# A macaron block on one core: order of transposes, copies and preparation in the attention loops

## Chip, cores, metric

The kernel runs on one core of a Trainium2 chip. The metric is the device time of one execution in microseconds; the median of three runs counts.

## The reference

The input x has 8 batches of 1024 tokens with 128 features, in f32. Three parts follow one another: half a feed-forward part (FFN), causal attention, and half an FFN again with the same weights.

```python
x = x + 0.5 * ffn(layernorm(x))
x = x + attention(layernorm(x))
x = x + 0.5 * ffn(layernorm(x))

def attention(z):                       # per batch, D = 128, 1024 tokens
    Q, K, V = z @ Qw, z @ Kw, z @ Vw
    s = Q @ K.T / sqrt(D) + causal_mask
    return softmax(s) @ V

def ffn(z):                             # 16 experts of 64, 4 chosen per token, one shared of 128
    cw = routing weights (sigmoid scores, groups, top 4, scaled)
    return sum_e cw[:, e] * (relu(z @ W1[e].T) ** 2 @ W2[e].T) + relu(z @ Ws1.T) ** 2 @ Ws2.T
```

## The kernel before

Each engine has one program, written out by hand; engines meet only by semaphores. An FFN runs over 16 groups of 512 tokens and 9 chunks of hidden units each. Most products are split into three f32r products (`split3`, lines 1371 to 1375). The second FFN's first groups (0 to 3) are prepared during the attention by `start_ffn(k)`, with k = 8(b-6) + s.

The attention runs over batches b = 0..7, and each batch has 8 slots s. Slot s handles the query tile t = `ORDER[s]` of (7, 3, 6, 2, 5, 1, 4, 0), each tile being 128 queries wide against (t+1)*128 keys. The even slots hold the wide tiles 7, 6, 5, 4 (`LATE`), the odd ones the narrow tiles 3, 2, 1, 0 (`SOON`). In a slot:

- TensorE writes the scores (`score`, L1567), into one of two PSUM homes; it waits for the exp of two slots before.
- VectorE takes the row maximum (`row_max`, L1246 or L1244), and L1248 shifts it for wide tiles.
- ScalarE takes the exp with its row sum (`exp`, L759).
- For a wide tile ScalarE casts the probabilities to f16 (`prob_hi`, an L572 copy into `shared`), GpSimd writes the remainder (`prob_lo`, L544), and SP transposes both by DMA (`prob_transpose` of SP, L352) into `wb`. TensorE uses them in `pair` (L1610 to L1612).
- For a narrow tile TensorE transposes the f32 probabilities (`prob_transpose`, L1585) into one PSUM bank, `tp_ps`, and ScalarE copies them out (`pT_copy`, an L572 copy into `w_raw`). Each transpose waits for the copy of the one before. TensorE uses the four tiles in `mix` (L1594), which the next batch's first `pT_copy` waits for, since it overwrites their home.

The results of `mix` and `pair` are copied (`uT_copy`, into `s_sb`), multiplied by Vw (`values`, L1626) and added to x on VectorE (`finish`, L1284). Beside this each loop prepares the next batch: transposes of the normalised tokens (L1559), `z_hi_copy` and `z_lo_part`, the product with Qw Kw^T (`q_product`, the `m_hi` rows of L1373 to L1375), `q_hi_copy` and `q_lo_part`, and ScalarE normalises the batch after next (`normalise` of the attention, L779, four instructions a half).

ScalarE's `start_ffn` does, for the FFN groups: half of the normalising (L586), `x_copy` (into `x_f`), `x_hi_copy` (into `x_hi`), a sigmoid by exp (L623) and `wT_copy` (into `wT`). Copies of all kinds stand on L572, so they are told apart by their tiles. TensorE's `start_ffn` transposes the normalised group (L1404), makes the logits (L1412) and transposes the routing weights (L1432). SP stores and spreads these (L363, L380), in the same queue as the DMA transposes. k = -22 to -19 fall in b=3, -14 to -11 in b=4, 0 to 7 in b=6 and 8 to 15 in b=7.

Of the kernel before, what the change touches and what calls it, by code (L numbers as in the profile page):

```python
# [118 lines left out]
def macaron_kernel(nc, x, Qw, Kw, Vw, Wg, bias_corr, W1, W2, Ws1, Ws2, out):  # L119
    B, S, D = x.shape  # L120
# [8 lines left out]
    QT = S // P  # L129
# [18 lines left out]
    with ExitStack() as ctx:  # L148
# [75 lines left out]
        SOON = ORDER[1::2]  # L224
# [346 lines left out]
        def _(sc):  # L571
# [157 lines left out]
            def attention(close_ffn, start_ffn, lead_ffn):  # L729
# [66 lines left out]
                def run():  # L796
                    for b in range(B):
                        for s in range(QT):
                            if b == 0 and s == 0:
                                close_ffn()  # L800
                            if b > 0 and s == 0:
                                pT_copy(b - 1, SOON[2])
                            if b > 0 and s == 2:
                                pT_copy(b - 1, SOON[3])
                            if b > 0 and s == 4:
                                uT_copy(b - 1, 1)
                            if b > 0 and s == 6:
                                uT_copy(b - 1, 0)
                            if b + 1 < B and s in (0, 2):
                                z_hi_copy(b + 1, s // 2, prep_ps)  # L810
                            exp(b, s)
                            if s in (5, 6):
                                pT_copy(b, SOON[s - 5])
                            if b + 1 < B and s in (4, 6):
                                q_hi_copy(b + 1, (6 - s) // 2, prep_ps)
                            if b + 2 < B and s == 4:
                                normalise(b + 2, 1)
                            if b + 2 < B and s == 6:
                                normalise(b + 2, 0)
                            if s % 2 == 1:  # L820
                                prob_hi(b, ORDER[s - 1])
                            start_ffn((b - (B - 2)) * QT + s)

                    pT_copy(B - 1, SOON[2])
                    pT_copy(B - 1, SOON[3])
                    start_ffn(16)
                    for r in range(3):
                        sc.wait_ge(A.p16_in[r], 16 * B)
                    lead_ffn(0)
                    lead_ffn(1)  # L830
                    uT_copy(B - 1, 0)
                    start_ffn(17)
                    lead_ffn(2)
                    uT_copy(B - 1, 1)
                    lead_ffn(AHEAD - 1)
# [532 lines left out]
        def _(pe):  # L1368
# [183 lines left out]
            def attention(close_ffn, start_ffn, lead_ffn):  # L1552
# [92 lines left out]
                def run():  # L1645
                    pe.wait_ge(m_ready, 1)
                    for b in range(B):
                        new = b + 1 < B
                        for s in range(QT):
                            if b > 0 or s > 1:  # L1650
                                score(b, s)
                            if b == 0 and s == 0:
                                close_ffn()
                            if s == 0:
                                if new:
                                    wait(pe, A.qlo_done[0], b + 1)
                                    z_transpose(b + 1, 0, prep_ps)
                                if b > 0:
                                    pair(b - 1, PAIRS[0], HQ, PAIRS[0] + 2)
                            if s == 1 and b > 0:  # L1660
                                prob_transpose(b - 1, SOON[3])
                            if s == 1 and b > 1:
                                values(b - 2, 0)
                            if s == 2 and new:
                                pe.wait_ge(A.zlo_done[0], b + 2)
                                z_transpose(b + 1, 1, prep_ps)
                            if s == 3 and b > 0:
                                pair(b - 1, PAIRS[1], 0, PAIRS[1] + 2)
                            if s == 4 and new:
                                q_product(b + 1, 1, prep_ps)  # L1670
                            if s == 5:
                                if b > 0:
                                    mix(b - 1)
                                prob_transpose(b, SOON[0])
                            if s == 6:
                                if new:
                                    pe.wait_ge(A.qlo_done[1], b + 2)
                                    q_product(b + 1, 0, prep_ps)
                                prob_transpose(b, SOON[1])
                                if b > 0:  # L1680
                                    values(b - 1, 1)
                            if s == 7:
                                prob_transpose(b, SOON[2])
                                pair(b, PAIRS[0], 0, HQ)
                            start_ffn((b - (B - 2)) * QT + s)

                    b = B - 1
# [56 lines left out]
```

## Time and profile before

| | us |
|---|---|
| median of 3 runs | 685.28 |
| the three runs | 685.28, 686.0, 681.53 |
| the profiled execution: its own time | 686.61 |
| its span | 684.8 |
| TensorE busy | 640.4 (94%) |
| VectorE busy | 559.1 (82%) |
| ScalarE busy | 549.7 (80%) |
| GpSimd busy | 521.7 (76%) |

The attention loops lie between about 278 and 446 us of the span. In a timeline row the columns are start, length, engine, line, operation, tiles written and read, shapes and the number of merged instructions; in brackets stands the engine's idle time before it and what ended it. The lengths of matmuls include a modelled end, so that the next often starts before it.

### The profile page before, as it was taken

Reading aid. Unit: us, or ns where it says so; the run is one execution under the profiler, and the core shown is the slowest. Engines: PE = TensorE matmul, PEld = TensorE weight load, DVE = VectorE, ACT = ScalarE, POOL = GpSimd, SP = SyncE. Lnnn points to the kernel's source line nnn. Section 1 sums busy time; section 2 is a strip of 40 time slices with the busy share of each in tenths; the row PEclk is TensorE's granted clock in tenths of the full one; section 3 lists DMA queues with packets and bytes.
Section 4 is the critical chain, followed back from the end, with each engine's and each line's share of the span. In section 5 each row is a group of like instructions: output and inputs, shape, how many; then the busy total and the mean of one; then the engine's idle time right before and its main releaser. Section 6 shows DMA issues by size and latency. Waiting matters only on the chain.

```text
span 684.8 us, 15211 instructions
## 1 busy us (share of the span) xinstructions
PE 640.4 (94%) x3395; PEld 493.8 (72%) x3395; DVE 559.1 (82%) x2576; ACT 549.7 (80%) x1171; POOL 521.7 (76%) x411
## 2 busy tenths in 40 slices
PE   4689999999999997699998998999999999999997
PEld 3457777777777765578776886777777777777775
DVE  5888989989899897767767768779889889898863
ACT  3478879898888874778887786769888898988975
POOL 3378889899998885665655546558899998999975
PEclk9699999999999999999999999999999999999999
DMA  9866677865777650334544435886867878768782
GB/s 245 194 139 128 140 160 151 167 130 129 161 158 165 134 124 1 59 74 76 96 81 78 74 76 96 162 161 123 171 143 159 176 170 174 160 142 187 167 172 76
DMA packets 107801, 92.05 MB, mean 134 GB/s; under 512 B 59488, under 2 KB 73456, under 8 KB 107760
## 3 DMA queue, kind: packets, MB, share of 16 engines
q1 hardware_dynamic: 105552, 91.00, 63.6%
q10 hardware_dynamic: 2208, 0.59, 0.4%
q8 instruction: 16, 0.26, 0.2%
q14 instruction: 25, 0.20, 0.1%
HBM read 72.70 MB, written 5.24 MB: 114 GB/s over the span
## 4 chain that ended last, share of the span: by engine, by line
PE 69%; DVE 13%; ACT 6%; issue 6%; DMA 3%; POOL 2%; SPq 0%; POOLq 0%; ACTq 0%; DVEq 0%
PE psum L1373 18%; PE psum L1374 17%; PE psum L1375 17%; PE psum L1446 3%; DVE w_raw L1246 3%; DMA wb<-scratch 2%; PE psum L1404 2%; PE psum L1458 2%; DVE zn L1272 1%; PE psum L1420 1%; DVE s_sb L1100 1%; PE psum L1412 1%; PE psum L1610 1%; ACT s_sb L759 1%; PE psum L1612 1%
## 5 line engine op out<-in xcount | busy, mean ns | idle before, releaser
L452 POOL TENSOR_TENSOR shared_r<-shared,shared_r 128x512 fp32r<-128x512 f32 x256 | 326.6, 1298 | 57.7 <-ACT shared L642 55.1
L1100 DVE SCALAR_TENSOR_TENSOR s_sb<-psum,wb 128x512 f32<-128x512 f32 x256 | 175.6, 687 | 47.4 <-DMA wb<-scratch 22.4
L641 ACT ACTIVATE shared_r<-s_sb 128x512 fp32r<-128x512 f32 x256 | 160.0, 625 | 46.3 <-DVE s_sb L1100 43.0
L642 ACT ACTIVATE shared<-s_sb 128x512 f32<-128x512 f32 x288 | 177.6, 619 | 20.0 <-DVE s_sb L1100 20.0
L1373 PE MATMUL psum<-x_hi,w_hi 128*128 128x512 f32 x288 | 126.3, 439 | 1.2 <-issue 0.9
L1373 PE MATMUL psum<-shared_r,w_hi 128*128 128x512 f32 x256 | 115.6, 452 | 1.2 <-POOL shared_r L452 1.0
L1375 PE MATMUL psum<-x_hi,w_lo 128*128 128x512 f32 x288 | 114.2, 396 | 0.0
L1374 PE MATMUL psum<-x_lo,w_hi 128*128 128x512 f32 x288 | 114.0, 396 | 0.0
L1374 PE MATMUL psum<-shared_r,w_hi 128*128 128x512 f32 x256 | 101.7, 397 | 0.0
L1375 PE MATMUL psum<-shared_r,w_lo 128*128 128x512 f32 x256 | 101.0, 395 | 0.0
L544 POOL TENSOR_TENSOR shared<-s_sb,shared 128x1024 f16<-128x1024 f32 (+3 forms) x32 | 56.7, 1771 | 44.3 <-ACT shared L572 44.3
L1373 PEld LDWEIGHTS psum<-x_hi,w_hi 128*128 128x128 f32 x288 | 54.7, 190 | 21.9 <-issue 8.2
L1374 PEld LDWEIGHTS psum<-x_lo,w_hi 128*128 128x128 f32 x288 | 54.6, 190 | 18.1 <-issue 7.2
L1375 PEld LDWEIGHTS psum<-x_hi,w_lo 128*128 128x128 f32 x288 | 54.5, 189 | 11.9
L1373 PEld LDWEIGHTS psum<-shared_r,w_hi 128*128 128x128 f32 x256 | 48.7, 190 | 19.2 <-issue 5.7
L586 ACT ACTIVATE xn<-x_sb,shift,roots 128x128 f32 (+1 forms) x128 | 55.4, 481 | 3.7 <-DVE shift L939 3.7
L1375 PEld LDWEIGHTS psum<-shared_r,w_lo 128*128 128x128 f32 x256 | 48.3, 188 | 11.6
L1374 PEld LDWEIGHTS psum<-shared_r,w_hi 128*128 128x128 f32 x256 | 49.0, 191 | 4.7 <-issue 0.2
L471 POOL TENSOR_TENSOR roots<-powers,neg_half 128x8 f32<-128x8 f32 x28 | 46.0, 1641 | 7.8 <-DVE powers L1080 5.5
L1246 DVE TENSOR_REDUCE w_raw<-psum 128x1 f32<-128x1024 f32 (+3 forms) x32 | 32.6, 1020 | 22.5 <-PE psum L1579 22.3
L458 POOL TENSOR_TENSOR x_lo<-x_f,x_hi 128x512 fp32r<-128x512 f32 x32 | 41.6, 1299 | 7.2 <-ACT x_hi L572 7.2
L759 ACT ACTIVATE s_sb<-psum,w_raw 128x1024 f32<-128x1024 f32 (+3 forms) x32 | 30.6, 955 | 16.3 <-DVE w_raw L1248 16.3
(170 smaller groups left out, 1372.3 us busy)
## 6 DMA issues: line engine op xcount, KB each, us to landing
wb<-scratch SPq DMA_DIRECT2D x128, 512.0 KB, 7.9
out<-x_sb SPq DMA_DIRECT2D x16, 256.0 KB, 9.9
x_sb<-in_L_attn_x SPq DMA_DIRECT2D x4, 256.0 KB, 6.2
scratch<-wT SPq DMA_DIRECT2D x32, 32.0 KB, 1.9
w_raw<-in_L_ffn_W ACTq DMA_DIRECT2D x1, 512.0 KB, 6.0
w_raw<-in_L_ffn_W SPq DMA_DIRECT2D x1, 512.0 KB, 6.6
wb<-shared SPq DMA_TRANSPOSE x32, 4.1
w_raw<-in_L_ffn_Ws ACTq DMA_DIRECT2D x1, 64.0 KB, 8.7
```

The costliest lines, as they stand in the source:

```text
L452: nc.gpsimd.tensor_tensor(g_lo[:, j % RING, :], g_f[:, j % RING, :], g_hi[:, j % RING, :].bitcast(F32), ALU.subtract).then_inc(F.glo_done, 1)
L458: nc.gpsimd.tensor_tensor(x_lo[:, u, :], x_f[:, u, :], x_hi[:, u, :].bitcast(F32), ALU.subtract).then_inc(F.xlo_done, 1)
L471: nc.gpsimd.tensor_tensor(roots[:], powers[:], neg_half[:, 0:2 * TG], ALU.pow).then_inc(F.rstd_done, 1)
L544: nc.gpsimd.tensor_tensor(prob16[t][:, :, 1, :], whole, prob16[t][:, :, 0, :], ALU.subtract).then_inc(A.plo_done, 1)
L586: ins = nc.scalar.activation(xn[:, t, :], x_sb[:, bass.ds(g * TG + t, 1), :].rearrange("p t d -> p (t d)"), ACT.Identity, bias=shift[:, t: ...
L641: nc.scalar.activation(g_hi[:, j % RING, :], s_sb[:, j % RING, :], ACT.Square)
L642: nc.scalar.activation(g_f[:, j % RING, :], s_sb[:, j % RING, :], ACT.Square).then_inc(F.sq_done, 1)
L1100: ins = nc.vector.scalar_tensor_tensor(s_, h_, 0.0, wb[:, u, c, :], ALU.max, ALU.mult)
L1246: nc.vector.tensor_reduce(raw_max[:, t:t + 1], src, AX.X, ALU.max, negate=True).then_inc(A.raw_max_done, 1)
L1373: mm(out_, l_hi, r_hi, start=start, stop=False)
L1374: mm(out_, l_hi, r_lo, start=False, stop=False)
L1375: return mm(out_, l_lo, r_hi, start=False, stop=stop)
```

## The change

On TensorE the transposes of tiles 3 and 2 stand first behind the scores of slots 5 and 6: ahead of `mix`, and ahead of the wait for and the work of `q_product`. On ScalarE the copy of tile 2 stands ahead of slot 6's exp instead of behind it, and `start_ffn` stands ahead of the attention's `normalise` and of `prob_hi` instead of behind them. No instruction is added or removed.

```diff
@@ ScalarE, attention, run @@
-                            if b > 0 and s == 6:
-                                uT_copy(b - 1, 0)
+                            if s == 6:
+                                if b > 0:
+                                    uT_copy(b - 1, 0)
+                                pT_copy(b, SOON[1])
                             if b + 1 < B and s in (0, 2):
                                 z_hi_copy(b + 1, s // 2, prep_ps)
                             exp(b, s)
-                            if s in (5, 6):
-                                pT_copy(b, SOON[s - 5])
+                            if s == 5:
+                                pT_copy(b, SOON[0])
                             if b + 1 < B and s in (4, 6):
                                 q_hi_copy(b + 1, (6 - s) // 2, prep_ps)
+                            start_ffn((b - (B - 2)) * QT + s)
                             if b + 2 < B and s == 4:
                                 normalise(b + 2, 1)
                             if b + 2 < B and s == 6:
                                 normalise(b + 2, 0)
                             if s % 2 == 1:
                                 prob_hi(b, ORDER[s - 1])
-                            start_ffn((b - (B - 2)) * QT + s)
@@ TensorE, attention, run @@
                             if s == 5:
+                                prob_transpose(b, SOON[0])
                                 if b > 0:
                                     mix(b - 1)
-                                prob_transpose(b, SOON[0])
                             if s == 6:
+                                prob_transpose(b, SOON[1])
                                 if new:
                                     pe.wait_ge(A.qlo_done[1], b + 2)
                                     q_product(b + 1, 0, prep_ps)
-                                prob_transpose(b, SOON[1])
                                 if b > 0:
                                     values(b - 1, 1)
```

## Rows read from the trace of the kernel before

**Rows 1.** Busy time by stage, the loop of b=3: stretch and length, then each engine.
```profile
337.12:359.70 22.58, 21.06 (x149) 17.12 (x147) 16.48 (x59) 18.45 (x42) 13.22 (x11) 1.00 0.40 76
```
**Rows 2.** Waits of TensorE, 278 to 450 us: total, times, longest.
```profile
PE psum L1585 <- ACT w_raw L572: 5.7, 9, 1.0
...
PE psum L1412 <- ACT x_f L572: 2.0, 3, 0.8
```
**Rows 3.** Timeline of TensorE, b=2, slots 6 and 7.
```profile
329.26 0.48 PE L1373 MATMUL psum<-z_hi,m_hi 128*128 128x512 f32 x1
...
330.09 0.52 PE L1585 MATMUL psum<-ident,shared 128*128 128x128 f32 x3
330.45 1.06 PE L1626 MATMUL psum<-vw,s_sb 128*128 128x128 f32 x8
...
332.47 0.41 PE L1585 MATMUL psum<-ident,shared 128*128 128x128 f32 x2 [0.61 <-ACT w_raw L572]
```
**Rows 4.** Timeline of ScalarE, b=2, the copies pT3 and pT2.
```profile
329.36 0.58 ACT L572 ACTIVATE w_raw<-psum 128x512 f32<-128x512 f32 x1
...
331.82 0.50 ACT L572 ACTIVATE w_raw<-psum 128x384 f32<-128x384 f32 x1
```
**Rows 5.** Timeline of TensorE, b=3, slots 5 to 7.
```profile
346.56 2.38 PE L1594 MATMUL psum<-w_raw,zn 128*128 128x512 f32 x8
348.77 0.60 PE L1585 MATMUL psum<-ident,qk_all 128*128 128x128 f32 x4
350.21 1.06 PE L1412 MATMUL psum<-wgT,x_f 128*128 128x16 f32 x8 [0.84 <-ACT x_f L572]
...
354.91 0.41 PE L1585 MATMUL psum<-ident,shared 128*128 128x128 f32 x2 [0.17 <-ACT w_raw L572]
```
**Rows 6.** Timeline of ScalarE, b=3: normalising, the x copy, pT3.
```profile
348.04 1.64 ACT L779 ACTIVATE zn<-x_sb,w_raw 128x128 f32<-128x128 f32 x4
349.57 0.58 ACT L572 ACTIVATE x_f<-psum 128x512 f32<-128x512 f32 x1
...
350.50 0.60 ACT L572 ACTIVATE w_raw<-psum 128x512 f32<-128x512 f32 x1
```
**Rows 7.** TensorE in b=0, then stages; behind POOL the granted clock.
```profile
289.78 0.52 PE L1585 MATMUL psum<-ident,shared 128*128 128x128 f32 x3 [0.87 <-ACT w_raw L572]
...
291.67 0.59 PE L1585 MATMUL psum<-ident,shared 128*128 128x128 f32 x2 [1.02 <-ACT w_raw L572]
...
281.52:284.93 3.41, 1.87 (x11) 1.59 (x11) 2.65 (x6) 2.62 (x6) 2.58 (x3) 1.00 0.01 2
...
288.35:291.76 3.41, 1.52 (x11) 1.01 (x10) 1.01 (x3) 3.41 (x9) 1.32 (x1) 1.00 0.61 113
291.76:295.17 3.41, 3.41 (x16) 2.57 (x17) 0.69 (x1) 3.02 (x9) 2.62 (x4) 0.50 0.59 113
```
**Rows 8.** b=6 and b=7: TensorE, ScalarE, DMA transposes of tiles 6 and 4.
```profile
419.08 0.41 PE L1585 MATMUL psum<-ident,shared 128*128 128x128 f32 x2 [0.90 <-ACT w_raw L572]
...
440.69 0.41 PE L1585 MATMUL psum<-ident,shared 128*128 128x128 f32 x2 [0.91 <-ACT w_raw L572]
...
450.99 0.27 PE L1610 MATMUL psum<-wb,zn 128*128 128x256 f16 x1
...
442.88 0.60 ACT L572 ACTIVATE x_f<-psum 128x512 f32<-128x512 f32 x1 [1.36 <-PE psum L1404]
...
L352 SPq DMA_TRANSPOSE wb<-shared x1: 2543/2543/2543, 435.5 to 435.5; - x1
DMA to landing us min/median/max: 5.1/5.1/5.1
...
L352 SPq DMA_TRANSPOSE wb<-shared x1: 1922/1922/1922, 443.0 to 443.0; - x1
DMA to landing us min/median/max: 6.1/6.1/6.1
```
**Rows 9.** The page's DMA issues: KB each, median us from issue to landing.
```profile
wb<-scratch SPq DMA_DIRECT2D x128, 512.0 KB, 7.9
```

## The prediction

> **What bounds the kernel now.** I read the page first. Its busy shares and its slices (TensorE 94%, a slice near 0.9 almost everywhere) say that TensorE sets the pace of both feed-forward parts and that the attention between them is where it has gaps. Then the busy time of one attention loop: the loop of batch b=3 takes 22.58 us of which TensorE is busy 21.06, ScalarE 18.45 and VectorE 16.48 [rows 1]. So no engine is full and TensorE comes nearest. There are eight such loops and the change touches only them. Next the waits of TensorE between 278 and 450 us: the transposes wait for a copy out of their PSUM bank nine times, 5.7 us in all, and the FFN logits wait for the copy of x three times, 2.0 us [rows 2]. Those two rows are what the change can reach. All else it can do only by making something earlier that TensorE then uses.
>
> I name the slots of a loop by s=0..7. The narrow tiles' transposes are T3 (tile 3, s=5), T2 (tile 2, s=6), T1 (tile 1, s=7) and T0 (next loop), their ScalarE copies pT3, pT2, pT1, pT0. One PSUM bank holds each in turn, so T2 waits for pT3 and T1 for pT2.
>
> **Change 1, T3 ahead of mix (s=5): 0 by itself.** pT3 also waits for mix (it overwrites what mix reads), so pT3 starts when both are done, as before. TensorE does the same work in another order.
>
> **Change 2, T2 ahead of the q product and pT2 ahead of exp (s=6).** Take b=2, which has no FFN work in these slots. Before: q product at 329.26, T2 at 330.09, values at 330.45, then TensorE runs free and sits idle 0.61 until T1 at 332.47, which pT2 released [rows 3]; pT2 starts at 331.82 and ends at 332.32 [rows 4] behind an exp. After: T2 would start at 329.26, but pT3 runs from 329.36 to 329.94 [rows 4], and the distance from a copy's end to the released matmul is 332.47 - 332.32 = 0.15 us. So T2 starts at 330.09 again, and 330.09 - 329.26 = 0.83 us of wait stands before it. The same work (q product, T2, values, score 7) that began at 329.26 and ended at 332.47 - 0.61 = 331.86 now begins 0.83 later and ends at 332.69. A matmul that waits for nothing starts about 0.16 before the modelled end of the one before it (T2 started at 330.09 with 0.52, the next at 330.45) [rows 3], so T1 starts at about 332.5. pT2 no longer waits for the exp, so it ends before 332.32 and is no longer the last. T1 moves from 332.47 to 332.5: nothing. A wait of 0.6 is removed and one of 0.8 is put before T2, against 0.2 of overlap that the stall hid. The stall stays, since pT3 is set by ScalarE's own row of work (exp, q copy, four normalisings, exp), which the change does not shorten. The same holds for b=1 and b=5. Bounds for the three loops: between a loss of 0.2 and a gain of 0.2 each; I take 0.
>
> In b=0 there is no mix and no values product. T2 stands at 289.78 and T1 at 291.67, with waits of 0.87 and 1.02 [rows 7]. T2 keeps its time (pT3), then q product 0.83, score 7 about 0.43: T1 at about 291.4. Gain 0.3 (0 to 0.6).
>
> **Change 3, the next stage's preparation ahead of normalise (b=3, b=4, s=4).** The logits of FFN group 0 wait 0.84 us for the x copy [rows 5], which starts at 349.57 behind four normalisings of 1.64 us from 348.04 [rows 6]. Now the copy starts at 348.04 and ends near 348.6. mix (346.56, 2.21 us to T3 at 348.77) and T3 (0.36) are done at 349.13 [rows 5], so the logits start there instead of at 350.21: 1.08 earlier, because T3's modelled end hid 0.24. From there to the end of score 7 TensorE took 354.91 - 0.17 - 350.21 = 4.53 us [rows 5]. In the new order about 0.1 comes on top, a wait of T2 for pT3 (350.50 to 351.10 [rows 6], which ScalarE's sum of work leaves where it is): the end is at 349.13 + 4.63 = 353.76, T1 about 0.16 before that, 353.6 against 354.91. Gain 1.3, of which the removed stall before T1 is a part. What is late next is pT3, not the logits. ScalarE's normalising is only 0.6 later and its reader is the next loop but one. b=4 repeats b=3 with the same two waits (0.84 and 0.17): 1.3 again. The times behind T1 in the next loop are led by TensorE and VectorE chains that start from its scores, so I let the gain stand. Bounds: 0.4 to 1.4 each.
>
> **Change 4, the last two loops (b=6, b=7).** Here preparation is moved not past normalise (there is none) but past the odd slots' half-precision copy of the wide probabilities, prob_hi. Gain side: T1 of b=6 waits 0.90 [rows 8]; with pT2 ahead of exp about 0.55 of it goes, and since VectorE leads the start of b=7, I count 0.4. T1 of b=7 waits 0.91 and could come 1.1 earlier. But the pair product right behind it needs the DMA transpose of tile 6, issued at 435.5 and landed 5.1 later, 440.6, while T1 stands at 440.69 [rows 8]. So that gain is hidden by the transfer. Loss side: x_hi of group 1 (a 512-wide copy as that at 442.88, 0.60 us) [rows 8] goes ahead of prob_hi of tile 7 and pushes GpSimd's chain, hence that transpose, back by 0.5. And in the last slot the x copy of group 3, which waits for TensorE until 442.88 [rows 8], goes ahead of prob_hi of tile 4. The transpose of this tile was issued at 443.0, GpSimd's 1.4 us and the cast's 0.7 after the cast's start near 440.8. Now the cast starts near 443.5, so prob_hi, GpSimd's low part, SP's DMA transpose (landed 6.1 after its issue, 449.1 [rows 8]) and SP's last load of routing weights queued behind it all move by about 2.7. Landing at 449.1 + 2.7 = 451.8 against the pair product's start at 450.99 [rows 8]: up to 0.8 late. In b=6 half the normalising of group 2 likewise goes ahead of prob_hi of tile 4; its transpose is used only in slot 3 of the next loop, and I put the loss inside the bounds. Together b=7 loses 0.5 (from a loss of 2.5, if the transpose meets the weight loads, to a gain of 0.4).
>
> The Trainium skill (page "TensorE: Matmul & The Clock Gate", section "Architectural detail: the array is 16× 32×32, not 1× 128×128") says ScalarE takes its queue strictly in order while TensorE can pull weight loads ahead. By that rule the blocked x copy holds all behind it, and change 4 has its loss; were it not so, the loss would be 0 and the sum 3.3.
>
> **Sum**: 0.3 + 0 + 1.3 + 1.3 + 0.4 - 0.5 = 2.8 us. The profiled execution took 686.61 us (span 684.8), so its like would take 683.8. The median of the runs shown is 685.28, 1.3 below the profiled one, so I predict 685.28 - 2.8, about 682.4.
>
> **The clock.** Between 288.35 and 291.76 TensorE was busy 1.52 us, with the two waits of b=0 in it, and the clock of the next stretch, to 295.17, was 0.50, that is 1.2 GHz; the stretch from 281.52, with 1.87 us busy, was followed by full clock, 2.4 GHz [rows 7]. The change takes the second of the two waits away. If the low stretch goes with it, its 3.41 us of work take half: 1.7 less. I leave it out of the sum: these rows show one case, and not that the wait was its cause.
> The same page of the Trainium skill ("HAM oscillation — how this bites in real kernels") has the clock fall after one long idle gap. Here it fell after waits of at most 1.02 us [rows 7], so the trace does not bear the rule out; by the rule there would be nothing to win, by the rows 1.7.
>
> **Rivals.** (a) The low stretch goes: 682.4 - 1.7 = 680.7. For it: TensorE does more just before it. Against: the first wait stays and grows. (b) The gains of b=3 and b=4 are eaten by later waits, above all TensorE's for VectorE in the next loop: both at their lower bound of 0.4, 1.8 less, 684.2. For it: VectorE carries routing work in b=4; against: its chain starts from TensorE's first score. (c) Slower: the blocked ScalarE queue in b=7. If the delayed transpose (issued at 445.7) runs beside the 512 KB weight loads and takes as long as these do, 7.9 us [rows 9], it lands at 453.6, 2.6 after the pair product was due; the last weight load, behind it on SP, is then needed as much later and costs nothing more. With x_hi's 0.5, and nothing won in b=6, 3.1 are lost against the gains of 0.3 + 2.6: 685.28 + 0.2 = 685.5. It decides from a landing at 453.4; every microsecond beyond that is one more. (d) Before T2 of b=0 the idle time now stands in one piece, 0.87 + 0.83 [rows 3, 7], and the clock falls for one more stretch: 682.4 + 1.7 = 684.1.
>
> **Chances.** Forecast (681.5 to 683.5) 0.50; (a) 0.20; (b) 0.15; (c) 0.07; (d) 0.08. The runs of the kernel before lie 4.5 us apart, so the range must take more than the terms: 679.3 to 685.9, with all four rivals in it. One per cent is 6.9 us, about what a measurement of this kernel tells from no change. The waits that the change reaches [rows 2] sum to 7.7 us, so faster by over 1% needs nearly all of them and the clock: 0.05. Slower by over 1% needs twice rival (c): 0.03. Within 1%: 0.92.
>
> **What would show it.** Right: the T1 waits on the copy are gone in all eight loops and a wait of 0.6 to 0.9 stands before T2 in b=1, 2, 5; the logits' wait of 0.84 is gone in b=3 and b=4, whose loops are 1.0 to 1.3 shorter; loops 1, 2 and 5 are as long as before; prob_hi of tile 4 in b=7 starts behind the x copy, near 443, and its transpose lands within 1 us of the pair product. Wrong: loops 1, 2 and 5 get shorter by over 0.3 (then pT3 is not what holds T2), or loop 7 with the start of the second FFN grows by over 1.5.

## The result, and the profile after

| | before | after |
|---|---|---|
| median of 20 runs each, taken side by side | 685.0 | 679.94 |
| lowest and highest | 681.2 to 687.84 | 677.11 to 682.79 |
| the profiled execution: its own time | 686.61 | 682.48 |
| its span | 684.8 | 680.7 |

The ratio is 0.994, with a 95% interval of 0.9923 to 0.9957: about 4.1 us less, where 2.8 were forecast. (It is formed from the means, 684.24 and 680.0; the medians are 5.06 apart.) The two profiled executions are also 4.1 apart (686.61 - 682.48), so their traces can be set against each other. All times are in us.

Busy times by engine, from the page after, are within 1.2 us of those before (TensorE 641.5, VectorE 558.4, ScalarE 549.4, GpSimd 521.8): nothing was removed, the time is idle time.

To find the place I measured each loop from the start of its first exp (tile 7) to that of the next; the last one up to the product of the second FFN that follows TensorE's wait of 0.85 to 0.88 behind the attention's last work (457.56 before, 453.51 after). This table is worked out from those starts, for all kernels of this study:

| kernel | b=0 | 1 | 2 | 3 | 4 | 5 | 6 | 7 |
|---|---|---|---|---|---|---|---|---|
| before | 20.30 | 19.33 | 19.81 | 22.58 | 23.95 | 19.87 | 21.31 | 32.73 |
| after | 20.08 | 19.20 | 19.71 | 21.06 | 22.55 | 19.79 | 20.42 | 33.10 |
| e1_preparation_only | 20.29 | 19.30 | 19.83 | 21.47 | 22.84 | 19.87 | 20.57 | 33.28 |
| e2_transposes_only | 21.13 | 19.21 | 19.71 | 22.09 | 23.54 | 19.78 | 21.30 | 33.24 |
| e3_t2_behind_q | 17.94 | 18.78 | 19.04 | 20.97 | 22.44 | 19.09 | 20.43 | 33.40 |
| e4_k7_behind | 21.03 | 19.21 | 19.72 | 21.07 | 22.54 | 19.78 | 21.31 | 33.02 |
| e5_xhi_behind | 19.72 | 19.23 | 19.72 | 21.06 | 22.54 | 19.77 | 20.44 | 32.42 |
| e6_t2_behind_q_xhi | 17.94 | 18.75 | 19.05 | 20.97 | 22.45 | 19.11 | 20.44 | 32.61 |
| e7_norm_late | 17.86 | 19.46 | 19.60 | 21.19 | 22.69 | 19.62 | 21.10 | 33.05 |
| e8_t3_behind_mix | 18.13 | 20.82 | 19.71 | 21.08 | 22.55 | 19.79 | 20.43 | 33.10 |
| e9_norm_two_inputs | 19.62 | 19.23 | 19.71 | 21.13 | 22.61 | 19.77 | 21.38 | 32.96 |
| e10_norm_strided | 18.16 | 19.21 | 19.70 | 21.07 | 22.54 | 19.78 | 21.32 | 32.98 |
| e11_pt2_only | 18.73 | 18.80 | 19.05 | 22.13 | 23.59 | 19.14 | 21.31 | 33.84 |
| e12_best_xcopy_behind | 17.94 | 18.77 | 19.05 | 20.97 | 22.44 | 19.09 | 20.43 | 33.25 |

Loops 1 to 6 repeat within 0.1 wherever their code is the same (but for one DMA wait in e8's loop 1), so a tenth can be read from a single profile. Loop 0 can't be read so; its part is told further down. After against before, loop by loop: 0.22, 0.13, 0.10, 1.52, 1.40, 0.08, 0.89, -0.37, together 3.97; with 0.08 before the attention this is the 4.1.

The loop of b=3 by engine (compare [rows 1], 22.58 with TensorE busy 21.06) is 1.52 shorter:
```profile
336.59:357.65 21.06, 20.56 (x150) 17.08 (x147) 16.50 (x59) 18.33 (x42) 12.99 (x11) 1.00 0.47 82
```
TensorE's waits of after, 275 to 450 us (total, times, longest), against [rows 2]:
```profile
...
PE psum L1587 <- ACT w_raw L572: 4.0, 5, 1.7
PE psum L1406 <- DVE x_sb L1286: 2.0, 2, 1.5
PE psum L1612 <- DMA wb<-shared: 0.8, 1, 0.8
PE psum L1434 <- DVE scw L1090: 0.8, 1, 0.8
...
```
Line numbers of TensorE's program and of VectorE's stand two higher than before. The transposes now wait five times instead of nine, and all five are T2's; no T1 waits for pT2 any more. The logits' wait for the copy of x is gone. The last two rows are new, both in b=7.

b=2, slots 6 and 7 of after, first TensorE, then ScalarE (against [rows 3, 4]):
```profile
329.67 0.52 PE L1587 MATMUL psum<-ident,shared 128*128 128x128 f32 x3 [0.67 <-ACT w_raw L572]
329.94 0.48 PE L1375 MATMUL psum<-z_hi,m_hi 128*128 128x512 f32 x1
...
331.96 0.39 PE L1587 MATMUL psum<-ident,shared 128*128 128x128 f32 x2
...
328.94 0.59 ACT L572 ACTIVATE w_raw<-psum 128x512 f32<-128x512 f32 x1
...
330.63 0.50 ACT L572 ACTIVATE w_raw<-psum 128x384 f32<-128x384 f32 x1
```
Counted from the loop's start (316.88 after, 317.31 before) T2 starts at 12.79, before at 12.78; T1 at 15.08, before at 15.16. The wait moved from T1 to T2, as the prediction had it.

b=3, slots 5 to 7 of after, TensorE and ScalarE (against [rows 5, 6]):
```profile
346.48 2.32 PE L1596 MATMUL psum<-w_raw,zn 128*128 128x512 f32 x8
348.63 0.96 PE L1414 MATMUL psum<-wgT,x_f 128*128 128x16 f32 x8
350.71 0.52 PE L1587 MATMUL psum<-ident,shared 128*128 128x128 f32 x3
...
353.00 0.39 PE L1587 MATMUL psum<-ident,shared 128*128 128x128 f32 x2
...
347.50 0.60 ACT L572 ACTIVATE x_f<-psum 128x512 f32<-128x512 f32 x1
347.98 1.65 ACT L779 ACTIVATE zn<-x_sb,w_raw 128x128 f32<-128x128 f32 x4
```
The x copy ends at 348.10, before mix does, and the logits follow mix without a wait. T1 starts 16.41 into the loop, before 17.79.

### The profile page after: what moved, and what is told of

The parts are those of the page before. It is cut to its first block, busy times and chain, and to the rows that moved or that the text cites. A ratio compares the mean times of both kernels' runs of the same rounds, so it can differ in the third digit from the quotient of the medians.

```text
span 680.7 us, 15211 instructions
## 1 busy us (share of the span) xinstructions
PE 641.5 (94%) x3395; PEld 496.5 (73%) x3395; DVE 558.4 (82%) x2576; ACT 549.4 (81%) x1171; POOL 521.8 (77%) x411
## 4 chain that ended last, share of the span: by engine, by line
PE 74%; DVE 7%; DMA 5%; issue 5%; ACT 4%; POOL 3%; SPq 0%; POOLq 0%; DVEq 0%; ACTq 0%
PE psum L1375 19%; PE psum L1376 18%; PE psum L1377 18%; DMA wb<-scratch 3%; PE psum L1448 3%; PE psum L1406 2%; PE psum L1460 2%; PE psum L1628 1%; POOL shared L544 1%; PE psum L1422 1%; DVE w_raw L1248 1%; DVE zn L1274 1%; DVE s_sb L1102 1%; PE psum L1612 1%; PE psum L1587 1%
## 5 line engine op out<-in xcount | busy, mean ns | idle before, releaser
L641 ACT ACTIVATE shared_r<-s_sb 128x512 fp32r<-128x512 f32 x256 | 159.9, 624 | 45.1 <-DVE s_sb L1102 41.6
L544 POOL TENSOR_TENSOR shared<-s_sb,shared 128x1024 f16<-128x1024 f32 (+3 forms) x32 | 56.7, 1772 | 47.5 <-ACT shared L572 47.5
```

Of the source, the lines that this page charges most:

```text
L544: nc.gpsimd.tensor_tensor(prob16[t][:, :, 1, :], whole, prob16[t][:, :, 0, :], ALU.subtract).then_inc(A.plo_done, 1)
L641: nc.scalar.activation(g_hi[:, j % RING, :], s_sb[:, j % RING, :], ACT.Square)
```

## The experiments

**Which part of the change does it.** e1 is the kernel before with only the preparation (`start_ffn`) moved; e2 is the changed kernel with this one edit put back. The edit, as e1 has it:
```diff
                                 q_hi_copy(b + 1, (6 - s) // 2, prep_ps)
+                            start_ffn((b - (B - 2)) * QT + s)
...
                                 prob_hi(b, ORDER[s - 1])
-                            start_ffn((b - (B - 2)) * QT + s)
```


> Only start_ffn stands ahead of normalise and prob_hi; the transposes and pT2 stand as before the change. Theory (two parts, each with its own gain): the logits' wait of 0.84 goes in b=3 and b=4, but T1 still waits for pT2 behind the exp, so these loops win about 0.7 us each and not 1.5; loops 0, 1, 2, 5 as before the change (20.30, 19.33, 19.81, 19.87); b=7 keeps its loss of 0.4. In all about 1.0 to 1.5 us faster than before. Rival (the preparation alone carries the gain of b=3 and b=4, the transposes only fill a stall): loops 3 and 4 win 1.4 to 1.5 each, in all 3.

> Only T3, T2 and pT2 stand early; start_ffn stands as before the change. Theory: the logits' wait of 0.84 stays in b=3 and b=4, T2 there waits for pT3 no longer than the logits have already waited, T1 comes about 0.3 to 0.6 earlier; loop 0 wins 0.2, loops 1, 2 and 5 0.1 each, loop 6 0.4 to 0.9, and b=7 has no loss. In all 1.5 to 2.5 us faster than before. Rival (the transposes are a wash everywhere): nothing in any loop but 0, at most 0.5 in all.

Measured: e1 681.26 us median (12 runs), ratio 0.9971 (0.9951 to 0.999). e2 683.1 us, ratio 0.9996 (0.9978 to 1.0014). In b=3 and b=4 the preparation alone takes off 1.11 and 1.11, the transposes alone 0.49 and 0.41, both together 1.52 and 1.40: they add up to within 0.12. In b=1, 2 and 5 each is worth at most 0.12. And in b=6 nearly the whole gain comes with the preparation (20.57 in e1, 0.74 of 0.89), none with the transposes alone (21.30 in e2), where the prediction had it the other way round.

Both expectations missed in part. e1's 1.11 lies between its theory (0.7) and its rival (1.4 to 1.5). e2 was expected 1.5 to 2.5 us faster and isn't told from the kernel before: loop 6 wins nothing, and its last loop is 0.51 longer (33.24), where no loss was expected. The reason of the latter is met in b=7 below.

**T2's place against pT2's.** e3 is the changed kernel with T2 back behind the q product, pT2 still ahead of exp:
```diff
                             if s == 6:
-                                prob_transpose(b, SOON[1])
                                 if new:
                                     pe.wait_ge(A.qlo_done[1], b + 2)
                                     q_product(b + 1, 0, prep_ps)
+                                prob_transpose(b, SOON[1])
```


> The changed kernel with T2 back behind the q product on TensorE, pT2 still ahead of the exp on ScalarE. Theory (T2 is held by pT3, so standing first buys nothing and its wait of 0.46 to 0.73 in b=1, 2, 5 and 1.73 in b=0 delays the q product): the wait before T2 falls to under 0.1 in b=1, 2, 5, T1 comes 0.5 to 0.6 us earlier there, 0.4 earlier in b=0 and b=6; in all about 2 us faster than the changed kernel, some 6 faster than before. Rival (what helps is T2 being early, since pT2 follows it): T1 waits again for pT2, and the loops are as long as before the change, 19.3 and 19.8.

Later e11: the kernel before, with only the copy pT2 moved ahead of exp on ScalarE (the two hunks of the change at `pT_copy`), and nothing else.

> The kernel before, with one edit of the change alone: the copy pT2 ahead of exp of score 7. T3, T2 and the preparation stay where they were. Theory (the order on ScalarE alone does the work, T2's early place does nothing or costs): T1's wait (0.61 before) goes, no wait of 0.7 stands before T2, and loops 1, 2 and 5 are 0.4 to 0.7 shorter than before, at 18.8, 19.05 and 19.1 as in e3_t2_behind_q; loops 3 and 4 lose 0.4 to 1.5 too; in all 2.5 to 4 us less than before, ratio 0.994 to 0.997. Rival of the prediction's kind (pT3 holds all, so the place of pT2 is worth nothing): loops as before, ratio 1.0.

Measured: e3 676.29 us (6 runs), ratio 0.9906 (0.9882 to 0.9931). e11 682.42 us (10 runs; one of them took 2195 us and is left out of the comparison), ratio 0.9979 (0.9955 to 1.0002). TensorE in b=2 of e3, from the q product on:
```profile
323.62 0.48 PE L1375 MATMUL psum<-z_hi,m_hi 128*128 128x512 f32 x1
...
324.49 0.52 PE L1587 MATMUL psum<-ident,shared 128*128 128x128 f32 x3
...
326.09 0.40 PE L1587 MATMUL psum<-ident,shared 128*128 128x128 f32 x2
```
Neither T2 nor T1 waits, and in e11 the same three rows stand 0.82 and 1.60 apart, in e3 0.87 and 1.60 (326.55, 327.37 and 328.97). In e3 (its loop starts at 311.71) T2 stands at 12.78 again, since pT3 still releases it (it ends at 324.34, 0.15 ahead), but T1 at 14.38 instead of 15.08: the 0.83 of q product fills the time in which TensorE would idle before T2, and doesn't stand between T2 and T1. Loops 1 to 7 of e3 together are 1.67 shorter than those of the changed kernel, near the 2 that its text expects. e11 separates the two edits of slot 6. pT2 ahead of exp takes 0.53, 0.76 and 0.73 off loops 1, 2 and 5 (19.33, 19.81, 19.87 to 18.80, 19.05, 19.14). T2 ahead of the q product then gives back 0.41, 0.66 and 0.64 (e2: 19.21, 19.71, 19.78). What the change shows, 0.1 a loop, is the rest of these two. As a whole e11's time didn't come out as well as its loops: its last loop is 1.11 longer than before, and from there to the end its profiled execution, at 685.21 well above its own median, took 2.5 more than that of before (683.4 - 453.65 = 229.75, against 684.8 - 457.56 = 227.24). The first has its cause in VectorE and GpSimd, shown below with e12. (In e11 a stretch of 1.2 GHz also lies in that loop, from 422.11 to 425.52; e4 has one at the same place, and its last loop, 33.02, is as long as those of e9 and e10, 32.96 and 32.98, which have none.) The second I did not trace. So e11 as a whole missed the 2.5 to 4 us that its text expects.

**Is pT3 what holds T2?** e7 takes work from in front of pT3: half of the attention's normalising moves from slot 4 to slot 5, behind pT3.
```diff
-                            if b + 2 < B and s == 4:
+                            if b + 2 < B and s == 5:
                                 normalise(b + 2, 1)
```


> The changed kernel, T2 in front as there, but the four normalisings of slot 4 stand in slot 5 behind pT3 (1.64 us taken from in front of pT3). Theory (pT3, and with it T2, is set by ScalarE's sum of work in front of it): exp of slot 5 and pT3 come about 1 us earlier, the wait before T2 of 0.46 to 0.73 in b=1, 2, 5 goes, these loops win 0.4 to 0.7. Rival (pT3 is set by mix, which it waits for): pT3 moves by under 0.2 and the wait before T2 stays.

Measured: 678.17 us (4 runs), ratio 0.991 (0.9879 to 0.994), which overlaps that of the change. T2's waits are gone in b=1, 2 and 5, so it was ScalarE's work ahead of pT3 that made them. The wait came back at T1, which waits 1.07 in b=0 and 0.56 to 0.57 in b=1, 2 and 5. TensorE's T1 and ScalarE's pT2 in b=2:
```profile
328.53 0.41 PE L1587 MATMUL psum<-ident,shared 128*128 128x128 f32 x2 [0.57 <-ACT w_raw L572]
...
327.91 0.47 ACT L572 ACTIVATE w_raw<-psum 128x384 f32<-128x384 f32 x1
```
T1 again starts 0.15 behind the end of its copy. ScalarE carries the same sum of work up to pT2, so the loops stay within 0.3 of those of the changed kernel (loop 6 is 0.68 longer, with a wait for a DMA transpose in it), and the 0.4 to 0.7 a loop that the text expects did not come.

**T3's place.** e8 is the changed kernel with T3 behind mix again.

> The changed kernel with T3 back behind mix. Theory (pT3 waits for both, so their order is worth nothing): every loop as in the changed kernel within 0.1 us (19.20, 19.71, 21.06, 22.55, 19.79, 20.42). Rival (T3 in front lets pT3 start earlier): loops 1, 2 and 5 longer by 0.3.

Measured: 680.47 us (1 run). Loops 2 to 7 are those of the changed kernel within 0.02: the forecast of 0 for this edit holds. (Loop 1 has 1.51 of waiting for a DMA transpose at 299.32, behind the short loop 0.)

**Where b=6 got 0.89.** e4 is the changed kernel with the preparation of one slot, k=7 (slot 7 of b=6), back behind `prob_hi` of tile 4:
```diff
-                            start_ffn((b - (B - 2)) * QT + s)
+                            k = (b - (B - 2)) * QT + s
+                            if k not in (7,):
+                                start_ffn(k)
...
                                 prob_hi(b, ORDER[s - 1])
+                            if k in (7,):
+                                start_ffn(k)
```


> The changed kernel with only k=7 (half the normalising of FFN group 2, in the last slot of b=6) back behind prob_hi. Theory (loop 6 won 0.5 more than forecast because GpSimd's prob_lo no longer runs beside VectorE's two normalisings, which took 1.35 us together before the change and 0.60 after it): these two take 1.3 again, and loop 6 takes about 20.9 instead of 20.42. Rival (the 0.5 is TensorE's, from T1): the two instructions may be slow or not, loop 6 stays at 20.4.

Measured: 681.16 us (1 run); loop 6 is 21.31, the whole 0.89 is gone, though T1 is still early. So by itself T1's wait was worth nothing there; with the preparation moved as well it was worth at most 0.15 (e1's 20.57 against 20.42). In the changed kernel, ScalarE, VectorE and GpSimd near the end of b=6:
```profile
417.90 0.88 ACT L586 ACTIVATE xn<-x_sb,shift,roots 128x128 f32<-128x128 f32 x2 [2.02 <-DVE shift L941]
...
420.41 1.11 ACT L759 ACTIVATE s_sb<-psum,w_raw 128x1024 f32<-128x1024 f32 x1 [0.74 <-DVE w_raw L1250]
...
417.90 0.60 DVE L956 TENSOR_SCALAR xn<-x_sb,roots,shift 128x128 f32<-128x128 f32 x2
...
418.97 1.22 DVE L1248 TENSOR_REDUCE w_raw<-psum 128x1 f32<-128x1024 f32 x1
...
419.48 1.41 POOL L544 TENSOR_TENSOR shared<-s_sb,shared 128x640 f16<-128x640 f32 x1 [1.81 <-ACT shared L572]
```
and in e4:
```profile
419.61 1.11 ACT L759 ACTIVATE s_sb<-psum,w_raw 128x1024 f32<-128x1024 f32 x1 [2.23 <-DVE w_raw L1254]
...
416.23 1.47 DVE L960 TENSOR_SCALAR xn<-x_sb,roots,shift 128x128 f32<-128x128 f32 x2
...
415.97 1.40 POOL L544 TENSOR_TENSOR shared<-s_sb,shared 128x640 f16<-128x640 f32 x1
```
Both kernels start VectorE's half of the normalising 17.9 into the loop (from 399.99 and 398.30). It takes 0.60 where GpSimd stands idle, as at the start of the kernel before (below), and 1.47 where GpSimd's low part of tile 4 is running: it ends 0.33 behind GpSimd's end (417.70 and 417.37), about the length of one of its two instructions. ```profile
7.61 0.60 DVE L954 TENSOR_SCALAR xn<-x_sb,roots,shift 128x128 f32<-128x128 f32 x2
```
Behind it, with no idle time of VectorE between, stands the row maximum of the first score of b=7, and the exp waits for that: 0.87 more in the pair, 0.89 more in the loop. In the changed kernel, ScalarE's half of that normalising goes ahead of `prob_hi` of tile 4 and waits 2.02 for VectorE's shift; `prob_hi` comes 2.9 later in the loop, and GpSimd's low part 1.8 later, out of VectorE's way.

Two more tried to take the normalising out of GpSimd's way while it stays beside it. Both are e4 with the four groups' normalising on VectorE written otherwise: e9 as scalar_tensor_tensor with the shift as a broadcast second input, e10 as the same tensor_scalar over even, then odd columns.
The line of e9, and below it that of e10, in place of the tensor_scalar:
```diff
+                        ins = nc.vector.scalar_tensor_tensor(xn[:, t, :], x_sb[:, g * TG + t, :], rstd[:, t:t + 1],
+                                                             shift[:, t:t + 1].to_broadcast([P, D]), ALU.mult, ALU.add)
```
```diff
+                        ins = nc.vector.tensor_scalar(xn[:, t, :].rearrange("p (a b) -> p b a", b=2),
+                                                      x_sb[:, g * TG + t, :].rearrange("p (a b) -> p b a", b=2),
+                                                      rstd[:, t:t + 1], shift[:, t:t + 1], ALU.mult, ALU.add)
```


> The changed kernel with x's copy of slot 7 in b=6 behind prob_hi, so that GpSimd's low part of tile 4 runs beside VectorE's normalising again (with tensor_scalar that pair took 1.47 us in e4_k7_behind, 0.60 in the changed kernel where GpSimd stood still, and loop 6 was 21.31 against 20.42). Here the four groups' normalising in attention is written as scalar_tensor_tensor with the shift as a second SBUF input. Theory A (a VectorE instruction with two SBUF inputs is locked out as well while GpSimd reads SBUF): the pair takes 1.3 us or more and loop 6 stays at 21.2 to 21.4. Theory B (only tensor_scalar's fast form is locked out): the pair takes 0.6 to 0.8 beside the low part of 1.40, loop 6 is 20.4 to 20.7, and the pairs in b=2, b=3 (1.33 and 1.50 in the changed kernel) and b=7 shrink likewise.

> As e9_norm_two_inputs, but the normalising stays a tensor_scalar with one SBUF input, and goes through its 128 columns with a step of two on both sides, even columns first. The values are the same. Theory A (it is the exclusion by GpSimd that makes the pair long, and only the contiguous form is subject to it): the pair takes at most 0.8 us beside GpSimd's low part of 1.40, and loop 6 falls from 21.31 to 20.4 to 20.6. Rival (GpSimd holds VectorE out whatever the form): 1.3 us or more, loop 6 stays at 21.3. Second rival (the pair's length isn't what sets loop 6): the pair is short and loop 6 stays at 21.3.

(The first text speaks of "x's copy of slot 7"; it is ScalarE's half of the normalising, as said above. Its pairs of 1.33 and 1.50 lie in b=3 and b=4.) Measured: 681.29 and 682.3 us (1 run each), loop 6 21.38 and 21.32. VectorE and GpSimd in e9:
```profile
415.94 1.54 DVE L961 SCALAR_TENSOR_TENSOR xn<-x_sb,roots,shift 128x128 f32<-128x128 f32 x2
...
415.67 1.41 POOL L544 TENSOR_TENSOR shared<-s_sb,shared 128x640 f16<-128x640 f32 x1
```
and in e10:
```profile
416.33 1.47 DVE L961 TENSOR_SCALAR xn<-x_sb,roots,shift 128x128 f32<-128x128 f32 x2
...
416.07 1.40 POOL L544 TENSOR_TENSOR shared<-s_sb,shared 128x640 f16<-128x640 f32 x1
```
For e9 theory A held: with the second SBUF input the pair took 1.54. For e10 theory A fell: a step of two doesn't free the instruction (1.47). Neither run separates the long pair from GpSimd's place; that the pair's length sets loop 6 rests on the chain of the two traces above and on all fourteen profiles of the table but one: where the pair takes 0.60, loop 6 is 20.4 to 20.6, and where it takes 1.35 to 1.54, it is 21.3 to 21.4. (The exception, e7, has another wait in b=6, 1.28 for a DMA transpose.)

**What costs in b=7.** e5 is the changed kernel with x_hi of group 1 (k=9) back behind `prob_hi` of tile 7; e6 has e5's and e3's edit; e12 is e6 with the last x copy (k=15) back behind `prob_hi` of tile 4 too. The diffs are e4's, with (9,), (9,) and (9, 15) in place of (7,).

> The changed kernel with only k=9 (x_hi of FFN group 1, slot 1 of b=7) back behind prob_hi of tile 7. Theory (the last loop is 0.37 longer, 33.10 against 32.73 us from its first exp to the second FFN's end of the wait, because GpSimd's chain behind prob_hi of tile 7 is 0.5 late, and with it the routing weights' transpose and the DMA transpose of tile 6): TensorE's wait of 0.79 for scw falls to 0.3, the pair product starts 0.35 to 0.5 earlier, and the last loop takes 32.7. Rival (the blocked x copy of the last slot makes it long): it stays at 33.1.

> T2 behind the q product and k=9 behind prob_hi, both on the changed kernel. Theory: the two gains add: loops 0 to 5 as with T2 behind q alone (17.9 to 18 where the clock stays at 2.4 GHz, 18.78, 19.04, 20.97, 22.44, 19.09), the last loop 0.4 shorter than its 33.40; some 9 us faster than before with the clock's part, at least 0.3 faster than T2 behind q alone. Rival for loop 0 (17.94 was a lucky place of the clock's stretches): a low stretch of 3.4 or more is there again and loop 0 takes 19.6 or more.

> e6_t2_behind_q_xhi (T2 behind the q product, x_hi of group 1 behind prob_hi of tile 7) with the last x copy (slot 7 of b=7) back behind prob_hi of tile 4 as well. In the changed kernel that copy waits 2.15 us for TensorE and holds prob_hi of tile 4 back, whose transpose was issued 2.94 us later in the loop than before. Theory (the delay costs nothing, since that transpose then lands 4.0 us after its issue instead of 6.1): prob_hi of tile 4 starts 2 to 3 us earlier in the loop, and the last loop stays at 32.6 or grows to 33.1 where GpSimd's low part of tile 4 comes to lie beside VectorE's routing work (as in e2_transposes_only, where an operation of 0.18 us took 1.40 there). Rival (c) of the prediction (the blocked ScalarE queue is what costs time in b=7): the last loop falls below 32.2. Time: 676 to 678.5 us, ratio 0.988 to 0.991, no better than e6_t2_behind_q_xhi; by the rival 0.985 to 0.988.

Measured: e5 678.94 us (10 runs), ratio 0.9914 (0.9885 to 0.9942); e6 676.5 us (6 runs), 0.9877 (0.9848 to 0.9906); e12 676.98 us (6 runs), 0.9894 (0.9866 to 0.9922). The changed kernel in b=7: TensorE, then ScalarE's x copy and GpSimd's low part of tile 4, then SP's transpose of that tile.
```profile
432.88 0.33 PE L1434 MATMUL psum<-ident,scw 128*128 128x128 f32 x1 [0.79 <-DVE scw L1090]
436.86 0.28 PE L1612 MATMUL psum<-wb,zn 128*128 128x256 f16 x1 [0.79 <-DMA wb<-shared]
...
438.81 0.60 ACT L572 ACTIVATE x_f<-psum 128x512 f32<-128x512 f32 x1 [2.15 <-PE psum L1406]
...
440.11 1.40 POOL L544 TENSOR_TENSOR shared<-s_sb,shared 128x640 f16<-128x640 f32 x1 [4.14 <-ACT shared L572]
...
L352 SPq DMA_TRANSPOSE wb<-shared x1: 1355/1355/1355, 441.5 to 441.5; - x1
...
DMA to landing us min/median/max: 4.0/4.0/4.0
```
TensorE's two waits of b=7 in e5:
```profile
429.51 0.33 PE L1438 MATMUL psum<-ident,scw 128*128 128x128 f32 x1 [0.28 <-DVE scw L1094]
433.33 0.28 PE L1616 MATMUL psum<-wb,zn 128*128 128x256 f16 x1 [0.63 <-DMA wb<-shared]
```
With x_hi behind, the wait for the routing weights falls from 0.79 to 0.28, that for the transpose of tile 6 from 0.79 to 0.63, and the last loop from 33.10 to 32.42: this edit of the change cost 0.68, more than its whole loss in b=7 (0.37). In e6 against e3 it is 0.79 (33.40 to 32.61).

The blocked x copy is another matter. e12 takes the block away (VectorE, GpSimd, SP's transpose of tile 4):
```profile
430.34 1.41 DVE L992 TENSOR_SCALAR scores<-scores 128x64 f32<-128x64 f32 x1
...
430.29 1.41 POOL L544 TENSOR_TENSOR shared<-s_sb,shared 128x640 f16<-128x640 f32 x1 [1.40 <-ACT shared L572]
...
L352 SPq DMA_TRANSPOSE wb<-shared x1: 1353/1353/1353, 431.7 to 431.7; - x1
...
DMA to landing us min/median/max: 6.6/6.6/6.6
```
and e6 has it:
```profile
430.60 0.18 DVE L992 TENSOR_SCALAR scores<-scores 128x64 f32<-128x64 f32 x1
...
433.34 1.40 POOL L544 TENSOR_TENSOR shared<-s_sb,shared 128x640 f16<-128x640 f32 x1 [4.19 <-ACT shared L572]
...
L352 SPq DMA_TRANSPOSE wb<-shared x1: 1441/1441/1441, 434.8 to 434.8; - x1
...
DMA to landing us min/median/max: 3.9/3.9/3.9
```
The loop starts at 413.87 in e12 and at 414.11 in e6. Without the block the transpose is issued 2.9 earlier in it (17.8 against 20.7) and lands only 0.2 earlier (24.4 against 24.6); TensorE uses it at 26.7 and 26.0 (440.55 and 440.16). And GpSimd's low part now starts 0.05 ahead of an instruction of VectorE's routing, which takes 1.41 instead of 0.18. Everything behind it on VectorE is late, ScalarE waits for it, and TensorE for ScalarE's copy:
```profile
437.86 0.63 ACT L641 ACTIVATE shared_r<-s_sb 128x512 fp32r<-128x512 f32 x1 [0.98 <-DVE s_sb L1106]
...
439.55 1.16 PE L1632 MATMUL psum<-vw,s_sb 128*128 128x128 f32 x8 [0.53 <-ACT s_sb L572]
```
In e6 ScalarE waits 0.15 at that place, and TensorE not at all. The last loop is 33.25 against 32.61. So taking the block away wins nothing here and costs 0.6, by the place that GpSimd's low part comes to lie in. What it would be worth without that meeting was not measured. Rival (c) is refuted for the changed kernel: there the transpose lands 1.4 ahead of its use (below). The same instruction of 0.18 takes 1.41 in e11's and 1.40 in e2's last loop. These are also long, 33.84 and 33.24, and have the same wait of TensorE, 1.33 and 0.41; in no other profile is there either.

**Loop 0 and the clock.** I set out to learn whether the low stretch goes with T1's wait. The same stretches of the loop in e8 (which starts it at 275.81), with TensorE's busy time first and the granted clock behind POOL:
```profile
283.97:287.38 3.41, 1.55 (x10) 1.05 (x7) 2.57 (x8) 3.41 (x10) 2.35 (x3) 1.00 1.01 192
287.38:290.79 3.41, 2.90 (x25) 2.67 (x25) 0.85 (x2) 3.41 (x8) 2.21 (x2) 1.00 0.35 59
```
and in e2 (start 275.35), where the clock falls at 286.92:
```profile
283.51:286.92 3.41, 1.57 (x10) 1.05 (x8) 2.59 (x8) 3.41 (x10) 2.36 (x3) 1.00 0.88 179
286.92:290.33 3.41, 2.88 (x12) 2.62 (x13) 0.02 (x1) 3.07 (x7) 2.21 (x2) 0.50 0.39 73
```
Both kernels have the same code in b=0 and TensorE did nearly the same before (1.55 and 1.57 busy, with the same waits up to there: 1.78, 1.55 and 0.65 in e8, 1.78, 1.53 and 0.65 in e2); in e8 the clock stays at 2.4 GHz, in e2 it falls to 1.2 GHz. b=0 has one code in seven profiles (after, e2, e4, e5, e8, e9, e10; T3's place differs only where there is a mix), and it took 18.13, 18.16, 19.62, 19.72, 20.08, 21.03 and 21.13. So the program alone doesn't decide it. In all profiles loop 0 is 17.9 to 18.2 with no low stretch in it and 18.7 to 20.3 with one of 3.4 us or, in the changed kernel, two; with one of 6.8 it is 21.0 to 21.1. With T2 behind the q product and the full change beside it there was none, in three profiles of three (e3, e6, e12: 17.94 each). That is too few to call it a cause; it stays open. What a low stretch costs is read from the same code at both clocks: 19.62 - 18.13, about 1.5 us, for one of 3.4 (e9, e8), and 21.13 - 18.13 = 3.0 for one of 6.8 (e2, e8).

## Why the prediction was right, and where it wasn't

The forecast of 2.8 us came out as 4.1, inside the wide range and under 1%. As a time it was less near: 682.4 was forecast and the median is 679.94, inside 679.3 to 685.9 but below the 681.5 to 683.5 that the forecast itself held, and nearest to rival (a)'s 680.7. Rival (a) is not what happened, though: the changed profile has two low stretches in loop 0 where the one before has one, and the granted clock of the 20 runs after averages 0.991, that of the runs of before taken beside the experiments 0.991 to 0.993. By steps, forecast and measured:

- **Change 1** (T3 ahead of mix): 0 and 0 (e8).
- **Change 2 in b=1, 2, 5**: 0, and 0.13, 0.10, 0.08. The working held to 0.1: T2 stands where it stood, and the wait went from T1 to T2. The waits before T2 are 0.46, 0.67 and 0.73, where 0.6 to 0.9 was said for all three; b=1 falls short of it. (The 0.83 was counted from start to start, and 0.16 of it is overlap.) What the prediction didn't see is that the 0 is a sum of two edits, -0.5 to -0.8 for the copy and +0.4 to +0.7 for the transpose.
- **Change 2 in b=0**: 0.3 and 0.22, but this says nothing, since one clock stretch more or less outweighs it. The changed profile had two in that loop, as rival (d) said, and e8 and e10 have none, as rival (a) said, with the same code there.
- **Change 3** (b=3, b=4): 1.3 each, and 1.52 and 1.40, at or just above the upper bound of 1.4. Forecast for T1 in b=3 was 353.6, from a loop start of 337.12: 16.48; it came at 16.41. The rest, 0.14, was gained behind T1, in the following loop's start. e1 and e2 show the two halves, the logits' wait (1.11) and T1's (0.4 to 0.5). The T2 wait of 0.1 that was put in did not come. Rival (b), that later waits eat the gain, is refuted by both loops.
- **Change 4, b=6**: 0.4 and 0.89, right in sign for the wrong reason, and this is the step that failed: "with pT2 ahead of exp about 0.55 of it goes, and since VectorE leads the start of b=7, I count 0.4". T1's wait goes, and by itself nothing comes of it (e2, e4: 21.30 and 21.31 against 21.31). The gain is made by the edit that was put down as a small loss, half the normalising of group 2 ahead of `prob_hi` of tile 4, because it moves GpSimd's low part off VectorE's normalising. That pair is no term of the prediction, though the trace of before shows it: it takes 0.60 at 7.61, and 1.34, 1.50, 1.35 and 1.93 in the attention, each time beside a GpSimd L544. So the sign of b=6 was luck.
- **Change 4, b=7**: -0.5 and -0.37. x_hi's push is right and a little larger (0.68 by e5). The late transpose was put at up to 0.8 late and came 1.4 early (landed at 445.5, used at 446.95). The failed term is the landing time: 6.1 was carried over from [rows 8], and it took 4.0. The landing was to be within 1 us of the pair product, and was not.

The sentence on ScalarE's strict order agrees with the trace in b=7: `prob_hi` of tile 4 stood behind an x copy that idled 2.15 for TensorE, and GpSimd idled 4.14. Only the price was wrong, since what hung on it was early enough.

The forecast misses 1.3 us, then: 0.5 in b=6, 0.3 in b=3 and b=4, 0.3 in b=1, 2, 5, and 0.1 in b=7, less 0.1 in b=0; the 0.1 left lies ahead of the attention.

The best version found is e6: T2 behind the q product, x_hi of group 1 behind `prob_hi`, all else as changed. Its interval (0.9848 to 0.9906) lies below that of the change (0.9923 to 0.9957). By their times e3 (0.9882 to 0.9931) and e12 aren't told from it; that e6 is ahead of both rests on the last loop of the profiles, 32.61 against 33.40 and 33.25.

## What to carry to other kernels

When a transpose waits for a copy out of a single bank, ask of every instruction between two such pairs on which side of the wait it stands: work that needs nothing belongs ahead of the transpose that will wait, and the copy ahead of everything on its own engine that isn't needed sooner. A change of such an order should be taken apart into its two engines' edits, since a zero can be the sum of a gain and a loss.

Before an instruction's length goes into a sum, look for the same one elsewhere in the trace; where two lengths occur, find out what ran on GpSimd beside the long one. Here the cost of a reordering on ScalarE came twice from where it put GpSimd's work, 0.9 in b=6 and 0.6 in b=7.

## What the runs showed of the hardware

**GpSimd holds up some of VectorE's instructions.** The pair of normalisings takes 0.60 with GpSimd idle, and 1.33 to 2.19 in the other three groups of the changed kernel, always beside an L544 of GpSimd. A tensor_scalar of 128x64 takes 0.18 or 1.41 (above). A tiny instruction with two inputs in SBUF does it too, in the changed kernel free and beside an L544 that began at 301.79:
```profile
343.57 0.15 DVE L1266 SCALAR_TENSOR_TENSOR w_raw<-w_raw 128x8 f32<-128x8 f32 x1
...
303.04 0.91 DVE L1266 SCALAR_TENSOR_TENSOR w_raw<-w_raw 128x8 f32<-128x8 f32 x1
```
Two kinds of VectorE's instructions that read PSUM don't show it. In the attention of the changed kernel the row maximum of 640 columns takes 0.81 to 0.82 in the seven cases where it starts with no GpSimd instruction running and 0.82 in the one where it starts beside one, and z_lo 0.68 in four and 0.68 to 0.69 in ten. In all the cases shown GpSimd's instruction started first and kept its own length (1.40 for 640 columns).

The Trainium skill (page "SBUF — State Buffer", section "Who interferes with whom") states this as an exclusive lock on one pair of SBUF ports, held for a whole instruction by whichever started first, and needed on VectorE's side by its two-port mode or by a second SBUF input. The traces agree in each of these cases, and e9 was a test of its second clause. By this rule the change is not a matter of ScalarE and TensorE alone, and the prediction should have weighed it.

**One DMA transpose landed at the same point of the loop, early issued or not.** The transpose of tile 4 in b=7 took 6.1 and 6.6 from issue to landing when issued 18.2 and 17.8 into the loop (before, e12), and 4.0 and 3.9 when issued 21.1 and 20.7 into it (after, e6). In before, e2, e5, e6, e11 and e12 it was issued 17.9 to 20.7 into the loop and landed at 24.3 to 24.6 in all six. I did not find out what it waits for.

**The clock falls with no long gap.** TensorE's waits in loop 0 of the changed kernel were 1.78, 0.58, 0.65 and 1.73, none longer, and two low stretches lie in it. The second and what stood before it, as in [rows 7]:
```profile
286.60:290.00 3.40, 1.32 (x7) 1.05 (x7) 2.16 (x5) 3.40 (x11) 2.20 (x3) 0.99 0.85 164
290.00:293.40 3.40, 3.29 (x14) 2.91 (x15) 0.44 (x2) 3.07 (x7) 2.55 (x3) 0.51 0.19 35
```
